# Attention: the second head group's halves exchanged, one key product and one turned query product for both groups in batches 1 to 3

## What is computed

```python
xh = layernorm(x).reshape(b, s, H, Dh)            # H = 8 heads of Dh = 16
q, k, v = xh @ Wq + bq, xh @ Wk + bk, xh @ Wv + bv
p = pos_encoding(s, e).reshape(s, H, Dh) @ Wp     # sines and cosines
content   = einsum('bqhd,bkhd->bhqk', q + u_bias, k)
pos_score = rel_shift(einsum('bqhd,khd->bhqk', q + v_bias, p))
attn = softmax((content + pos_score) / sqrt(e))
ctx = einsum('bhqk,bkhd->bqhd', attn, v).reshape(b, s, e) @ Wo + bo
```

## Time and profile before

| | us |
|---|---|
| runs of the kernel before (3) | 522.3, 524.16, 527.06 (median 524.16) |
| the profiled execution: its time | 526.05 |
| the profiled execution: its span | 524.3 |
| PE busy, share of the span | 466.4 (89%) |
| DVE busy | 364.0 (69%) |
| ACT busy | 275.2 (52%) |
| POOL busy | 255.1 (49%) |

### The profile page before, as it was taken

The page is one execution under the profiler, slowest core; times in us unless marked ns, Lnnn a source line. Parts: engine busy times, 40 slices in busy tenths (PEclk is TensorE's granted clock), DMA queues, the critical chain, the costliest instruction groups (busy, mean ns, idle before and its releaser), DMA issues.

```text
span 524.3 us, 9996 instructions
## 1 busy us (share of the span) xinstructions
PE 466.4 (89%) x3157; PEld 324.6 (62%) x3157; DVE 364.0 (69%) x902; ACT 275.2 (52%) x570; POOL 255.1 (49%) x270
## 2 busy tenths in 40 slices
PE   8899999999999999999887999969899797887760
PEld 7665666666767667666764799833456456366650
DVE  3987677687877787567555566479888876466752
ACT  2356567766676666457531455536564443154543
POOL 3462564457572873232304454532536687455650
PEclk9999999999999999679887999979999989898985
DMA  8399999999998000000030321082000000133105
GB/s 310 109 190 178 187 221 344 206 201 210 207 201 137 1 2 11 11 1 2 22 131 20 84 75 31 14 319 113 1 2 0 1 26 30 52 87 74 33 16 161
DMA packets 68403, 52.71 MB, mean 101 GB/s; under 512 B 3255, under 2 KB 66110, under 8 KB 67713
## 3 DMA queue, kind: packets, MB, share of 16 engines
q1 hardware_dynamic: 65376, 47.24, 42.5%
q0 software_dynamic: 2976, 4.85, 3.2%
HBM read 21.30 MB, written 32.09 MB: 102 GB/s over the span
## 4 chain that ended last, share of the span: by engine, by line
PE 67%; DVE 17%; issue 5%; ACT 4%; DMA 3%; POOL 2%; POOLq 0%; DVEq 0%; another core or an unknown queue 0%; ACTq 0%; SPq 0%
PE banks L1060 14%; PE banks L1198 8%; PE banks L1207 7%; PE banks L1042 6%; PE banks L1075 6%; PE banks L1031 5%; PE banks L1037 3%; PE banks L1254 3%; PE banks L1143 3%; DVE arena L1748 2%; DVE nmax L1495 2%; DVE xc L1740 1%; DVE z L1734 1%; PE banks L1130 1%; PE banks L1271 1%
## 5 line engine op out<-in xcount | busy, mean ns | idle before, releaser
L825 ACT ACTIVATE arena<-banks 128x512 f32<-128x512 f32 x128 | 76.3, 597 | 79.9 <-PE banks L1060 76.2
L1060 PE MATMUL banks<-ca,work 128*128 128x128 f32 x512 | 86.4, 294 | 5.1 <-ACT work L818 5.1
L818 ACT ACTIVATE work<-banks,nmax 128x512 f32<-128x512 f32 x128 | 80.7, 685 | 17.7 <-DVE nmax L1495 17.4
L1060 PEld LDWEIGHTS banks<-ca,work 128*128 128x128 f32 x512 | 56.2, 145 | 38.8 <-issue 24.9
L1495 DVE TENSOR_REDUCE nmax<-banks 128x2 f32<-128x1024 f32 x64 | 78.3, 1224 | 2.2
L1031 PEld LDWEIGHTS banks<-arena 32*128 32x128 f32 x256 | 42.6, 190 | 32.5 <-issue 25.3
L1042 PE MATMUL banks<-arena 32*128 32x512 f32 (+3 forms) x256 | 61.7, 443 | 0.0
L1031 PE MATMUL banks<-arena 32*128 32x128 f32 x256 | 57.0, 303 | 2.0 <-remote 1.4
L1483 DVE COPY_PREDICATED banks<-ca,banks 128x256 f32<-128x256 uint32 x64 | 27.2, 425 | 35.1 <-PE banks L1031 34.8
L1198 PE MATMUL banks<-t,arena 128*128 128x128 f32 x300 | 46.0, 290 | 5.0 <-DVE arena L1628 2.4
L1037 PE MATMUL banks<-arena 32*128 32x128 f32 (+2 forms) x192 | 46.3, 422 | 0.0
(11 more groups left out here) (241 smaller groups left out, 837.3 us busy)
## 6 DMA issues: line engine op xcount, KB each, us to landing
regions<-zeros SPq DMA_DIRECT2D x15, 1040.0 KB
regions<-zeros SPq DMA_DIRECT2D x9, 1032.0 KB, 19.1
arena<-wp_in SPq DMA_DIRECT2D x1, 4624.0 KB, 24.5
arena<-wp_in SPq DMA_DIRECT2D x1, 4494.0 KB, 16.5
arena<-ct_in SPq DMA_DIRECT2D x2, 1024.0 KB, 8.5
arena<-cb_in SPq DMA_DIRECT2D x1, 1660.0 KB, 6.8
arena<-regions SPq DMA_DIRECT2D x23, 65.0 KB
arena<-regions SPq DMA_DIRECT2D x20, 64.5 KB
```

Source lines behind the costliest of these rows:

```text
L818: eng.activation(prob[:, r, :], bank[r], ACT.Exp, bias=nmax[:, s % 2, jj:jj + 1]).then_inc(s_exp, 1)
L825: eng.activation(probT[:, v % 2, j0 + jj, :, i % 2 * P:(i % 2 + 1) * P], turned_in(s, jj).rearrange("p (t q) -> p t q", t=TB), ACT.Copy).t ...
L1060: mm = eng.transpose(turned_in(s, jj)[:, t * P:(t + 1) * P], prob[:, 2 * (s % 2) + jj, t * P:(t + 1) * P], ident)
```

## The change

The second group's halves are exchanged: its position part stands in the first 16 rows of each head, its content part in the last 16. With that the nonzero rows of the two groups' key weights are complementary, and so are those of the two m2. One weight `wk0` and one `m2_0` take both; in batches 1 to 3 there is one key product and one t2 product for both groups, and two DVE evictions of each (`keys` with a mask of rows, `turn_by` with the group's sine table), the second in a new event, `rest`, one step after the job. Batch 0 still makes its keys and queries group by group. The key bias goes into the tables (new POOL event `kt`). POOL exchanges columns of the weights on the chip (`swap`, five small copies, for which `bias` and `fold` wait, and one copy into `wk0` after batch 0's first key product). The second group's tables are loaded by eight transfers of 16 partitions in the place of one. In the list, batch 0's second group has its queries at steps 1 and 2 and its keys at step 3, where `kb` and `kt` now stand ahead of `xbo` and batch 1's `normz`; `kd` 1 moves behind the `delta` events; in batches 1 to 3, `q` of the first group and `corr` stand one step later.

```diff
-    for e in (("stats", 0), ("cols", 0), ("kd", 0), ("job", "pem", 0), ("job", "wqT", 0), ("normz", 0), ("job", "bias", 0),
+    for e in (("stats", 0), ("cols", 0), ("swap", 0), ("kd", 0), ("job", "pem", 0), ("job", "wqT", 0), ("normz", 0), ("job", "bias", 0),
               ("job", "zT", 0), ("job", "fold", 0), ("job", "k", 0, 0), ("kb", 0, 0), ("job", "t1a", 0, 0),
               ("job", "t2a", 0, 0), ("qa", 0), ("job", "corr", 0), ("delta", 0, 0), ("job", "t1r", 0, 0),
-              ("job", "t2r", 0, 0), ("kd", 1)):
...
+    put(("kd", 1))
+    put(("kt", 1))
     at(0, ("job", "v", 0))
-    at(1, ("job", "k", 0, 1), ("kb", 0, 1))
-    at(2, ("job", "t1", 0, 1))
-    at(3, ("job", "t2", 0, 1), ("q", 0, 1), ("xbo", 0))
+    at(1, ("job", "t1", 0, 1))
+    at(2, ("job", "t2", 0, 1), ("q", 0, 1))
+    at(3, ("job", "k", 0, 1), ("kb", 0, 1), ("kt", 0), ("xbo", 0))
...
         at(base + first, ("normz", b))
         at(base + first + 1, ("job", "zT", b))
-        at(base + first + 2, ("job", "k", b, 0), ("kb", b, 0))
-        at(base + first + 3, ("job", "k", b, 1), ("kb", b, 1))
+        at(base + first + 2, ("job", "k", b))
+        at(base + first + 3, ("rest", "k", b), ("kb", b, 0), ("kb", b, 1))
         at(base + 7, ("job", "t1", b, 0))
-        at(base + 8, ("job", "t2", b, 0), ("q", b, 0))
-        at(base + 9, ("job", "corr", b))
-        at(base + 10, ("job", "t1", b, 1))
-        at(base + 11, ("job", "t2", b, 1), ("q", b, 1))
+        at(base + 8, ("job", "t2", b))
+        at(base + 9, ("rest", "t2", b), ("q", b, 0))
+        at(base + 10, ("job", "corr", b))
+        at(base + 11, ("job", "t1", b, 1), ("q", b, 1))
         at(base + 13, ("job", "v", b), ("xbo", b))
...
+        def keys_of(b, g):
+            return after("k", *((b,) if b else (b, g)))
+
+        def turned_of(b, g):
+            return after("t2", b, g) if b == 0 else after("t1", b, 1) if g else after("t2", b)
+
+        def tables(g):
+
+            return s_ct[g], 16 * (2 * HG if g else 1)
+
+        def on(g, posn):
+
+            n = 0 if posn == (g == 0) else 1
+            return A("pmask")[:, n:n + 1]
+
+        def halves(v):
+            return v.rearrange("p (j h d) -> p j h d", j=HG, h=2)
...
                 mine = slice(g * WIDE_T // NG, (g + 1) * WIDE_T // NG)
-                eng.dma_start(ct[:, mine], ct_in[:, mine]).then_inc(s_ct[g], 16)
+                if g == 0:
+                    eng.dma_start(ct[:, mine], ct_in[:, mine]).then_inc(s_ct[g], 16)
+                else:
+
+                    for k in range(2 * HG):
+                        to, here = slice(k * DH, (k + 1) * DH), slice((k ^ 1) * DH, ((k ^ 1) + 1) * DH)
+                        eng.dma_start(ct[to, mine], ct_in[here, mine]).then_inc(s_ct[g], 16)
...
                     rsqrt(mv[:, 0, :, 1], rstd[:, 0, :], TB, 1.0, 1e-5, (s_var, variance[e]))
+                elif kind == "swap":
+
+                    eng.wait_ge(s_ca[0], 16)
+                    for k in range(2):
+                        eng.tensor_copy(halves(m1s)[:, :, k, :], halves(A("m1_1"))[:, :, 1 - k, :]).then_inc(s_swap, 1)
+                    for k in range(2):
+                        eng.tensor_copy(halves(turnm)[:, :, k, :], halves(A("ident"))[:, :, 1 - k, :]).then_inc(s_swap, 1)
+                    eng.tensor_copy(halves(A("m2_0"))[:, :, 0, :], halves(A("m2_1"))[:, :, 1, :]).then_inc(s_swap, 1)
+                elif kind == "kt":
+                    g = b
+                    eng.wait_ge(s_kd, g + 1)
+                    if g:
+                        eng.wait_ge(s_bk, 1)
+                        mine = col[:, 2:3]
+                    else:
+                        eng.wait_ge(s_ca[1], 16)
+                        eng.wait_ge(*after("k", 0, 0))
+                        mine = A("bk0")
+                    eng.tensor_scalar(T(f"ka{g}"), T(f"ka{g}"), mine, None, ALU.add).then_inc(s_kt, 1)
+                elif kind == "job" and jobs[b] == ("k", 0, 0):
+
+                    eng.wait_ge(s_ca[1], 16)
+                    eng.wait_ge(s_job, b + 1)
+                    eng.tensor_copy(halves(A("wk0"))[:, :, 1, :], halves(A("wk1"))[:, :, 0, :]).then_inc(s_wk, 1)
                 elif kind == "kd":
                     g = b
...
-                        for n, m in enumerate(("m1_0", "m2_0", "m1_1", "m2_1")):
-                            mm = eng.matmul(bk[:, n * P:(n + 1) * P], wqT, A(m), start=True, stop=True)
+                        eng.wait_ge(s_swap, 5)
+                        for n, m in enumerate((A("m1_0"), A("m2_0"), m1s)):
+                            mm = eng.matmul(bk[:, n * P:(n + 1) * P], wqT, m, start=True, stop=True)
                     elif name == "bias":
                         eng.wait_ge(*after("pem", 0))
                         eng.wait_ge(*after("wqT", 0))
                         eng.wait_ge(s_cols, 5)
-                        for n, m in enumerate(("m1_0", "m2_0", "m1_1", "m2_1")):
-                            eng.matmul(bk[:, n:n + 1], A(m), col[:, 0:1], start=True, stop=True)
                         eng.matmul(bk[:, 4:4 + H], wqT, pm1[:, :], start=True, stop=True)
-                        mm = eng.matmul(bk[:, 4 + H:4 + 2 * H], colB, pm1[:, :], start=True, stop=True)
+                        eng.matmul(bk[:, 4 + H:4 + 2 * H], colB, pm1[:, :], start=True, stop=True)
+                        eng.matmul(bk[:, 0:1], A("m1_0"), col[:, 0:1], start=True, stop=True)
+                        eng.wait_ge(s_swap, 5)
+                        eng.matmul(bk[:, 1:2], A("m2_0"), col[:, 0:1], start=True, stop=True)
+                        eng.matmul(bk[:, 2:3], m1s, col[:, 0:1], start=True, stop=False)
+                        mm = eng.matmul(bk[:, 2:3], turnm, col[:, 1:2], start=False, stop=True)
                     elif name == "zT":
                         eng.wait_ge(s_z, TB * (a[0] + 1))
                         for t in range(TB):
...
-                        mm = eng.matmul(bk, A(f"wk{a[1]}"), xnT[:, 0:S], start=True, stop=True)
+                        if a != [0, 0]:
+                            eng.wait_ge(s_wk, 1)
+                        mm = eng.matmul(bk, A("wk0"), xnT[:, 0:S], start=True, stop=True)
                     elif name == "v":
                         eng.wait_ge(*after("zT", a[0]))
+                        eng.wait_ge(s_bk, 1)
                         for t in range(TB):
                             mm = eng.matmul(bk[:, t * D:(t + 1) * D], xnT[:, t * P:(t + 1) * P],
                                             A("wv").rearrange("p (h d) -> p h d", h=H)[:, :, 0:DH],
                                             start=True, stop=True)
                     elif name[0] == "t":
-                        b, g = a
-                        eng.wait_ge(*after("zT", b))
+                        eng.wait_ge(*after("zT", a[0]))
                         eng.wait_ge(*after("fold", 0))
-                        n = 2 * g + (name[1] == "2")
+                        n = 1 if name[1] == "2" else 2 * a[1]
                         part = queries(name)
                         mm = eng.matmul(bk[:, part], wt[:, n * P:(n + 1) * P], xnT[:, part], start=True, stop=True)
                     elif name == "corr":
...
                         for t in range(TB):
                             mm = eng.matmul(bk[:, t * H:(t + 1) * H], xnT[:, t * P + 1:(t + 1) * P + 1],
                                             few[:, 4:4 + H], start=True, stop=True)
+                        if a[0] == 0:
+                            eng.wait_ge(s_ca[1], 16)
+                            eng.wait_ge(s_swap, 5)
+                            mm = eng.matmul(bk[:, TB * H:TB * H + 1], turnm, A("bk1"), start=True, stop=True)
                     elif name == "ctxT":
                         eng.wait_ge(s_cx, parts(a[0], a[1:]))
                         for t in tiles_of(a):
...
                 eng.reciprocal(sm[:, 4, :], total).then_inc(count(s_v), 1)
                 own()
+            def keys(b, g, bk, shown):
+
+                eng.wait_ge(s_kt, 1 if g else 2)
+                eng.scalar_tensor_tensor(out=ka[:, b % 2, g, :], in0=bk, scalar=on(g, False), in1=T(f"ka{g}"),
+                                         op0=ALU.mult, op1=ALU.add).then_inc(count(shown), 1)
+
+            def turn_by(table, g, dst, bk, bias, part, shown):
+
+                eng.wait_ge(*tables(g))
+                eng.scalar_tensor_tensor(out=dst[:, part], in0=bk[:, part], scalar=few[:, bias:bias + 1],
+                                         in1=T(f"{table}{g}")[:, part], op0=ALU.add, op1=ALU.mult).then_inc(count(shown), 1)
+
             for kind, *w in plan:
                 if kind == "cols":
                     eng.wait_ge(s_ca[0], 16)
                     eng.tensor_tensor(col[:, 0:1], A("bq"), A("v"), ALU.add).then_inc(count(s_cols), 1)
                     eng.memset(col[:, 4:8], 0.0).then_inc(count(s_cols), 1)
                     own()
...
```

(38 more changed lines are left out.)

36 lines of the change are left out of this document (20 added, 16 removed).

## The result

The kernel after took 529.01 us (median of 12 runs, 522.49 to 532.07) against 523.34 for the kernel before (12 runs, 520.5 to 529.93). The ratio, taken without the few runs that lie more than 1.5% above the fastest of their kernel, is 1.0101, with a 95% interval of [1.0072, 1.0129]: some 5.3 us slower (the medians of all runs lie 5.7 apart). On another chip it was 1.0092 [1.005, 1.0135]. The forecast was 527.6, which is 3.4 us slower than the median that it started from.

A forecast was written before the change was run, and what follows sets the result against it. PE was taken to bound the attention, DVE and waits about 15 to 45 us. Terms -5.16 + 0.35 + 5.2 + 2.7 + 0.2 + 0.15 = +3.4 on the median 524.16 gave 527.6 us, range 521.5 to 532.5.

The forecast's parts named there:

- POOL's queue in step 3: z waits behind kb, kt 0 and xbo; PE rests some 5.6 us and batch 1's zT starts 6.2 us later.
- The 0.97 behind `zT`: PE's old wait for an exponential behind batch 1's zT disappears after the rest, leaving a loss of 5.2 us.
- The clock: Half clock on PE behind the rest ahead of batch 1's zT, priced at 2.7 us.
- rival 2: The rest comes and half clock lasts as long as the longest row, 13.66 us: +6.4, 530.6 us; chance 0.18.
- Nearer to the 3.11 than to the 2.36: Choice of the middle clock price: idle 3.11 us had half clock for 6.85 us behind it, 2.36 had none.
- Rival 1: The rest ahead of zT comes but the clock holds: +0.7, 524.9 us; chance 0.2.
- The products: One key and one t2 product fewer in each of batches 1 to 3: 6 x 0.86 = 5.16 us off PE.
- The 0.35: Batch 1, step 6: numbers and second key eviction on DVE take 3.46 against 3.08, so 0.35 us is given back.
- The start: Before the first scores: 0.2 us for POOL's exchange copies and 0.15 for a DVE copy behind corr.
- The 0.2 for the exchange copies: PE's bias waits for POOL's five column copies at the start: 0.2 us, bounds 0 to 2.7.
- I count 0: Eight table transfers in place of one cost nothing at the start; without cover the first gate would be kd 1.
- The margin of `q`: Batch 1, first group's q one event later: its 1.04 us to spare shrinks to 0.3 to 1.0, price 0.

The follow-up runs named there:

- e1: Kernel after with xbo and normz of batch 1 ahead of kb and kt 0 on POOL in step 3; 517.46 us, ratio 0.9879 to before.
- e4: e1 with the eight narrow table transfers issued behind x's remainder; 515.88 us, ratio 0.9866 to before.
- f2: Kernel after with six unneeded 128x512 products on PE in front of batch 1's zT; 525.65 us, ratio 1.0037 to before.
- g2: Kernel after, unchanged, run and profiled again on another chip ("after again"); 526.78 us, ratio 1.0092 to before.
- f3: Kernel after with only the eight narrow table transfers moved behind x's remainder; 526.51 us, ratio 1.0043 to before.
- e3: Kernel after with the second group's table loaded by one transfer, halves not exchanged, so its scores differ from the reference; 525.65 us, ratio 1.0037 to before.
- e2: Kernel before with only batch 0's second group reordered (queries at steps 1 and 2, keys and kb at 3), no product removed; 528.85 us, ratio 1.0113.
- f4: e4 with batch 0's second group in the old order (keys at step 1, queries at 2 and 3), kt 0 behind z; 521.6 us, ratio 0.9932 to before.
- g1: Kernel before, unchanged, run and profiled again on a third chip; 521.48 us, ratio 0.9965 to before.
- f1: e4 with the shared key and t2 products of batches 1 to 3 each done twice; 522.7 us, ratio 0.9983 to before.
- g3: e4, unchanged, timed again on another chip; 514.4 us, ratio 0.9853 to before.

## Why the prediction was right, and where its terms were off

Stage by stage, forecast and measured (after; after again):

| term | forecast | after | after again |
|---|---|---|---|
| start, to score 3 | +0.35 | +1.77 | +1.46 |
| `zT` later, without the start | +6.2 | +6.25 | +6.23 |
| the wait behind `zT` recovered | -0.97 | -0.97 | -0.97 |
| batch 1's key product | -0.86 + 0.35 | -0.86 | -0.86 |
| the clock behind the rest | +2.7 | +3.76 | +4.21 |
| scores 10 to 52: five products | -4.3 | -4.07 | -4.00 |
| sum, to score 52 | +3.4 | +5.9 | +6.1 |

(The two lines of 0.97 and 0.86 are those with which the sums of e1, e4 and f2 come out to 0.05; the clock is what is left then.)

**POOL's queue in step 3: right.** The start was 1.77 late at score 3. Without that, DVE's query work ends at 35.0, the key eviction at 37.9, z at 45.1, and `zT` starts at 45.26; forecast were 35.0, 37.9, 45.15 and 45.2. The rest was forecast with 5.6 and measured with 5.60 or 5.61 in after, g2, f3 and e3; `kt` 0, taken from a row of the same size, was 1.56 for 1.57. e1 and e2 show that this order is both enough and needed for the loss.

**The 0.97 behind `zT` is recovered: right, but for another reason.** I put it down to the rest. e1 and e4 have no rest and no such wait, and f4, with the old order, has waits of 0.56 and 1.00 there: the wait went with the query work, which DVE now does a step earlier. So the new order is worth something by itself, which after can't show.

**The clock: right in kind, too small.** The price was that of a stretch of 6.85 us at 42% of its time. Behind rests of 5.6 the stretches were about 10.2 us, in all four executions, and cost 3.7 to 4.3; behind e2's rest of 4.05 it was 6.8 us and 3.1. This lies between the forecast and rival 2. "Nearer to the 3.11 than to the 2.36" chose the right side, but the length of the stretch was taken from a rest little more than half as long. The prediction also passed over a third long idle time in the trace of before, with 3.4 us of half clock behind it (timeline of PE, then busy times); by it the price would have been 3.42 x 0.42 = 1.4:

```profile
418.80 0.43 PE L997 MATMUL banks<-own,cb 128*128 128x56 f32 x2 [2.95 <-DVE upto_tile L1360]
```

```profile
419.57:422.99 3.42, 3.42 (x11) 2.22 (x10) 1.86 (x7) 0.39 (x2) 2.67 (x3) 0.50 0.11 38
```

So the rows bounded the price from 0 to 5.7 and did not single out the middle. The share of 42% held where it was read (5.85 of 13.66 us, or 43%, before against g1); behind the rests some 47% was lost. Rival 1 (the clock holds) is refuted. The rule of the Trainium skill ("TensorE: Matmul & The Clock Gate", "Why this matters for your kernels"), that an idle gap between bursts sends the clock to half, agrees with these four. What set off the 13.66 us of the earlier trace rows is not shown: PE has no idle time above 0.68 us in the 60 us ahead of it.

**The products: right.** Five of them gave 4.07 in after, 0.79 to 0.87 each at the steps where they stood, and f1 makes it 4.75 for six. The 0.35 that I gave back in step 6 shows at that step and does not last: in after the step to score 8 takes 3.35, against 3.02 where a key product is gone elsewhere, but the next one takes 3.62 in the place of 3.88, and the sums of e1, e4 and f2, taken at score 10, close without it.

**The start: the term that failed.** The 0.2 for the exchange copies can't be told from the spread: batch 0's `zT` starts at 9.03 in after and at 9.57 in g2, where PE waits 0.61 for the last of them, and without copies at 8.91 (before), 8.98 (g1) and 8.11 (e2). The wait for the table covers it. The failing step is "I count 0" for the table transfers, with "the first gate would be `kd` 1". The first gates are `kd` 0 and the first key eviction, and the table that they need is not one of the eight pieces but the wide one ahead of them on the same queue. It came later with eight narrow ones right behind it: first table at 11.88 to 14.39 in the four executions of that order (after, g2, e1, f2), at 9.91 to 11.88 with one wide transfer behind it (before, g1, e2, e3), at 10.52 to 11.25 with x's remainder behind it (e4, g3, f1, f3, f4). In time it is 0.6% (e3, f3), some 3 us, but 1.6 us and within the noise between e1 and e4, which differ by the same move; at score 3 the profiles say 1.2 to 1.4 (e3, f3), as single executions of a start that varies. So the sign is shown by e3 against after, and the size stays open, between about 1 and 3 us.

**The margin of `q`: right.** 0.68 of the 1.04 was left, inside the 0.3 to 1.0 forecast.

So the sign, the cause and its place came out as forecast, and two terms were too small: the start by 1.1 to 1.4, the clock by 1.1 to 1.5. That 527.6 lies within 1.4 us of the measured 529.01 is in part luck: it stands on a median of three runs, 0.8 above that of twelve, and in the difference the miss is some 2 us (+3.4 against 5.3). The ratio, 1.0101 and on the other chip 1.0092, lies at the 1% between the prediction's "within 1%" (0.64) and "slower by over 1%" (0.3), and does not decide between them. **Open** stays why narrow transfers delay the wide one in front of them, why one half-clock stretch lasts 3.4 and another 10.2, and where the 1 to 3 us lie by which most kernels are timed below their score 52.

## What to carry to other kernels

When an event moves in a list that every engine runs through in order, work out for each engine what now stands in front of the next batch's producer; here z stood behind a `kb` that had to wait for DVE, came 6 us late, and cost more than six products had brought, and two lines of order (e1) turned a loss of 1.0% into a gain of 1.2%. Price a rest of PE twice: its own length, and the half clock behind it, here 5.6 us and another 4. And put transfers that are needed late behind those that are needed early, even if each is small.

## What the runs showed that was not expected

Behind a late table half clock followed. Timelines of PE, in front of score 0, of after and of e1:

```profile
16.66 0.34 PE L1085 MATMUL banks<-arena 32*128 32x128 f32 x1 [1.27 <-DVE corr L1671]
```

```profile
18.25 0.55 PE L1086 MATMUL banks<-arena 32*128 32x128 f32 x1 [3.00 <-DVE corr L1672]
```

DVE's first work with the table is late, so `corr` is, and PE rests in front of the first score: 1.27 in after, 1.76 in e2, 3.00 in e1, 3.24 in f2. Half clock followed for 3.4, 6.8, 10.2 and 6.8 us. With 0.17 (before, g1) or no wait (e4, f1, f3, g2) there was none between 12 and 40 us. It is no clean line: e3 and f4 lost 3.4 us of clock behind 0.34 and 0.26, and g3 behind none that the timeline shows.

A single profile of this kernel can hold a half-clock stretch of 13.66 us that the next one lacks, worth 5.85 us: as much as the whole change. The starts of the same step in both profiles show where such a stretch lies; the spans don't.
